# Attention block on eight cores: another order of loads and projections at the start, roots of the last stage on VectorE and GpSimd, and another treatment of the last four token tiles

## The reference

```python
x = x + layernorm(attention(layernorm(x)))     # q, k, v, output projection Wp with bias bp
x = x + layernorm(layernorm(x) @ W[idx] + b[idx])   # idx = argmax(log_softmax(logits) + gumbel(u))
```

## Time and profile before

| | us |
|---|---|
| three timed runs: median (lowest to highest) | 788.21 (786.87 to 789.79) |
| the profiled execution | 792.3 |
| span of its slowest core, core 4 | 791.3 |
| spans of the eight cores | 775.4 to 791.3 |
| busy on core 4: TensorE, VectorE, ScalarE, GpSimd | 691.6, 432.2, 516.2, 116.3 |

### The profile page before, as it was taken

The page is one execution under the profiler, slowest core; times in us unless marked ns, Lnnn a source line. Parts: engine busy times, 40 slices in busy tenths (PEclk is TensorE's granted clock), DMA queues, the critical chain, the costliest instruction groups (busy, mean ns, idle before and its releaser), DMA issues.

```text
span 791.3 us, 17031 instructions; the slowest of 8 cores (775.4 to 791.3 us)
## 1 busy us (share of the span) xinstructions
PE 691.6 (87%) x5700; PEld 259.0 (33%) x5700; DVE 432.2 (55%) x778; ACT 516.2 (65%) x686; POOL 116.3 (15%) x214
## 2 busy tenths in 40 slices
PE   1679999999899999999999998999999999994663
PEld 1344333434333343333333332323233333331221
DVE  4162666664655463452432323476767677674597
ACT  2243126534488687888787888888888888884011
POOL 0110002122211311212111142011011011001000
PEclk9978888888899999999999999999999999998797
DMA  8798247735056132122400064212222322322122
GB/s 204 140 190 171 64 99 198 166 78 148 23 142 148 55 91 63 29 52 45 92 16 15 16 121 109 81 31 78 82 81 69 93 77 76 108 81 88 66 61 93
DMA packets 78627, 72.00 MB, mean 91 GB/s; under 512 B 58448, under 2 KB 60752, under 8 KB 78544
## 3 DMA queue, kind: packets, MB, share of 16 engines
q1 hardware_dynamic: 71856, 59.77, 28.1%
q0 software_dynamic: 6688, 11.14, 8.9%
HBM read 60.68 MB, written 8.52 MB: 87 GB/s over the span
## 4 chain that ended last, share of the span: by engine, by line
PE 61%; issue 14%; ACT 9%; DVE 7%; DMA 6%; POOL 1%; SPq 1%; ACTq 0%; DVEq 0%; POOLq 0%
PE sps L630 10%; PE pj L587 10%; PE pj L571 10%; PE yps L663 10%; ACT Pr L1006 8%; PE pj L580 8%; PE pj L606 4%; PE pj L615 4%; PE zps L681 4%; DMA zr<-zev 2%; DMA wkb<-wk 1%; DMA zscr<-zi 1%; DMA zb<-zscr 1%; DVE Vsb L729 1%; DVE xst L852 1%
## 5 line engine op out<-in xcount | busy, mean ns | idle before, releaser
L1006 ACT ACTIVATE Pr<-sps,negc 128x1024 bf16<-128x1024 f32 (+1 forms) x416 | 429.8, 1079 | 111.3 <-PE sps L632 107.7
L1051 POOL TENSOR_TENSOR Pr<-Pr,mk_sb 128x172 bf16<-128x172 bf16 x192 | 100.3, 543 | 530.0 <-ACT Pr L1006 529.9
L630 PE MATMUL sps<-QY,Ksb 64*128 64x512 bf16 (+2 forms) x480 | 137.7, 348 | 17.9 <-ACT Pr L1006 15.7
L632 PE MATMUL sps<-QY,Ksb 64*128 64x512 bf16 (+2 forms) x480 | 139.3, 352 | 0.0
L663 PE MATMUL yps<-Pr,Vsb 128*32 128x512 bf16 (+5 forms) x1920 | 126.6, 351 | 4.7 <-POOL Pr L1051 2.6
L606 PE MATMUL pj<-wpb,QY 128*128 128x512 bf16 x256 | 68.1, 397 | 16.7 <-DVE QY L820 11.4
L681 PE MATMUL zps<-Pr,cbf 128*32 128x512 bf16 (+2 forms) x960 | 82.2, 347 | 0.0
L630 PEld LDWEIGHTS sps<-QY,Ksb 64*128 64x128 bf16 x480 | 35.7, 94 | 124.9 <-issue 122.2
L580 PE MATMUL pj<-fmQ,wqb 128*128 128x512 bf16 x256 | 67.6, 414 | 1.3 <-ACT Ksb L985 0.7
L729 DVE TENSOR_TENSOR Vsb<-pj,bvb 128x512 bf16<-128x512 f32 x48 | 33.0, 687 | 57.6 <-PE pj L587 52.8
L571 PE MATMUL pj<-fmA,wkb 128*128 128x384 bf16 x256 | 56.1, 370 | 9.2 <-DMA wkb<-wk 6.0
(11 more groups left out here) (93 smaller groups left out, 681.1 us busy)
## 6 DMA issues: line engine op xcount, KB each, us to landing
xin<-xkv SPq DMA_DIRECT2D x21, 512.0 KB, 4.2
zb<-zscr SPq DMA_DIRECT2D x64, 128.0 KB, 2.9
xr<-xq SPq DMA_DIRECT2D x16, 512.0 KB, 3.4
out<-xr SPq DMA_DIRECT2D x16, 512.0 KB, 2.8
xin<-xq SPq DMA_DIRECT2D x12, 512.0 KB, 4.5
wkb<-wk POOLq DMA_DIRECT2D x2, 1024.0 KB, 16.0
wqb<-wq POOLq DMA_DIRECT2D x2, 1024.0 KB, 20.3
wvb<-wv POOLq DMA_DIRECT2D x2, 1024.0 KB, 18.2
```

The source lines that it names most:

```text
L630: PE.matmul(sps[s % 2][:, 0, off:off + w], Ksb[0:64, g, hp, kc:kc + 128], QY[0:64, t, hp, n0:n0 + w], start=True, stop=True, tile_position ...
L632: mm = PE.matmul(sps[s % 2][:, 1, off:off + w], Ksb[64:128, g, hp, kc:kc + 128], QY[64:128, t, hp, n0:n0 + w], start=True, stop=True, tile ...
L1006: A.activation(out=Pr[:, s % 4, :, 0:wide], in_=sps[s % 2][:, :, 0:wide], func=AF.Exp, bias=negc[:, k:k + 1], scale=0.125).then_inc(s_exp, 1)
L1051: op = G.tensor_tensor(out=view, in0=view, in1=mk[:, j:j + 1, :].broadcast_to([128, 2, BAND]), op=ALU.mult)
```

## The change

Lead: `wk` comes in row halves; `wv` is issued when token tile 3 has landed and `wq` when tile 6 has; tiles 3 to 5 are issued after `wk`, tiles 6 to 9 after `wv`. The units' order is K, eight V units, Q, four V units, and the lead's units rotate over four banks (`pj`, `yps`, `zps`). Last stage, tiles 0 to 11: the three roots of each tile are made from a bit guess (three one-column operations on VectorE) and three Newton steps (nine one-column operations on GpSimd). End, tiles 12 to 15: each has a pair of PSUM banks of its own; the biases enter the product as one more matmul from rows that GpSimd splits into bf16 parts; the seven chunks of O that need no last head are multiplied ahead; statistics and the residual read PSUM; `ln3` and the last pass are done on ScalarE; the store is made in halves. The last head's row sums go through ScalarE's DMA queue, and `zinv` and `ynorm` stand later in their lists.

```diff
-    out = t[:3] + k0[:2] + t[3:4] + k0[2:4] + t[4:5] + k0[4:6] + t[5:6] + k0[6:]
-    out += k1[:1] + t[6:7] + k1[1:3] + t[7:8] + k1[3:4] + [("N", "K", 0, 0)] + k1[4:5] + t[8:9] + k1[5:7] + t[9:]
-    out += k1[7:] + [("N", "K", 0, 1)] + q[:4] + [("N", "K", 1, 0)] + q[4:] + [("N", "K", 1, 1)]
-    out += v[:2] + [("N", "Q", 0, 0)] + v[2:5] + [("N", "Q", 0, 1)] + v[5:8] + [("C", 0)] + v[8:]
+    v0, v1 = [[("V", g, sc, eh) for sc in range(3) for eh in range(2)] for g in (0, 1)]
+    nk, nq = [("N", "K", g, h) for g in range(2) for h in range(2)], [("N", "Q", 0, h) for h in range(2)]
+    out = t[:3] + k0[:4] + t[3:4] + k0[4:6] + t[4:5] + k0[6:] + t[5:6] + k1[:3] + nk[:1] + k1[3:] + nk[1:2]
+    out += v0[:2] + t[6:7] + nk[2:3] + v0[2:4] + t[7:8] + nk[3:] + v0[4:] + t[8:9] + v1[:2] + t[9:]
+    out += q + v1[2:3] + nq[:1] + v1[3:4] + nq[1:] + v1[4:5] + [("C", 0)] + v1[5:]
...
-    end = o[12] + o[13] + o[14] + f[12] + o[15] + f[13] + f[14] + f[15]
-    return mid, end
+    return mid
...
-    ln = {i: 5.0 + 2.7 * i for i in range(10)}
+    ln = {i: [5.5, 8.2, 12.0, 26.0, 28.5, 31.0, 44.0, 47.0, 50.0, 53.0][i] for i in range(10)}
+    come = {("K", 0, 0): 20.0, ("V", 0, 0, 0): 44.0, ("Q", 0, 0): 60.0}
...
-    ln.update({10 + i: end["Q", 0, 7] - 2.0 + 4.0 * i for i in range(4)})
-    ln.update({14 + i: end["V", 1, 1, 1] + 4.0 * i for i in range(6)})
+    ln.update({10 + i: end["Q", 0, 7] + [-10.0, -7.0, -1.0, 2.0][i] for i in range(4)})
+    ln.update({14 + i: end["Q", 0, 7] + 6.0 + 4.0 * i for i in range(6)})
...
+    for i, s in enumerate(TAIL):
+        pe.append((NP + 2.0 + 0.1 * i, "tailo", s))
+        pe.append((NP + 3.0 + 0.1 * i, "tailf", s))
...
+                pool.append((x + 1.2 + 4.0, "zroot", u[1]))
+                dve.append((x + 1.2 + 5.5, "x1", u[1]))
+                pool.append((x + 1.2 + 10.0, "x1root", u[1]))
+                dve.append((x + 1.2 + 11.5, "ln3", u[1]))
...
+        by, late = (sp, 1.35) if k < 31 else (act, 1.0)
+        by.append((x + 1.4, "zrow", k))
+        dve.append((x + 4.2 * late, "zinv", k))
+        by.append((x + 4.6 * late, "zout", k))
+        by.append((x + 7.6 * late, "zback", k))
+        again = begin[LAST[k + 2] + 2] - 0.3 if k < 29 else begin[NP] + 20.0
+        dve.append((min(x + 13.5 * late, again), "ynorm", k))
...
+    at = begin[NP] + 16.0
+    z_at, x_at, f_at, last_at = [0.0, 1.4, 5.2, 9.0], [2.8, 6.6, 10.4, 12.8], [15.2, 18.6, 22.0, 26.0], [17.4, 21.0, 24.5, 28.3]
+    for j, s in enumerate(TAIL):
+        dve.append((at + z_at[j], "tailz", s))
+        act.append((at + z_at[j] + 1.4, "tailzroot", s))
+        dve.append((at + x_at[j], "tailx", s))
+        act.append((at + x_at[j] + 2.4, "tailln", s))
+        sp.append((at + x_at[j] + 4.5, "turn", s))
+        dve.append((at + f_at[j], "tailfs", s))
+        act.append((at + f_at[j] + 1.4, "tailfroot", s))
+        dve.append((at + last_at[j], "taillast", s))
+        act.append((at + last_at[j] + 0.6, "tailout", s))
+        sp.append((at + last_at[j] + 1.2, "tailstore", s))
+    for i in range(3):
+        pool.append((begin[FIRST[30]] + 1.0 + 9.0 * i, "biasrow", i))
...
+def bank_number(u):
+
+    return (UNIT_N[u] - 1) % (4 if UNIT_N[u] <= LEAD else 2)
...
+    tail_ps = [pjs[:], sps[0][:], sps[1][:], yzs[:]]
+
+
+    lead_banks = pj + [yps, zps]
...
+    def guess(st, sem_g, n):
+
+
+        V = nc.vector
+        V.tensor_scalar(out=st[:, 14:15], in0=st[:, 13:14], scalar1=EPS, scalar2=0.5,
+                        op0=ALU.add, op1=ALU.mult).then_inc(sem_g, 1)
+        V.wait_ge(sem_g, 3 * n + 1)
+        V.tensor_scalar(out=st[:, 15:16].bitcast(I32), in0=st[:, 14:15].bitcast(I32), scalar1=1, scalar2=None,
+                        op0=ALU.arith_shift_right).then_inc(sem_g, 1)
+        V.wait_ge(sem_g, 3 * n + 2)
+        V.tensor_scalar(out=st[:, 15:16].bitcast(I32), in0=st[:, 15:16].bitcast(I32), scalar1=-1.0,
+                        scalar2=float(0x5f3759df - (1 << 22) - (1 << 31)),
+                        op0=ALU.mult, op1=ALU.add).then_inc(sem_g, 1)
...
+        def tail_begin(s, eh):
+
+            bank = tail_ps[s - 12][:, eh, :]
+            PE.matmul(bank, bsel[:], brow[0][:, 512 * eh:512 * eh + 512], start=True, stop=False)
+            for c in range(7):
+                PE.matmul(bank, QY[:, 3, c, 128 * (s - 12):128 * (s - 11)],
+                          wpb[:, c, 512 * eh:512 * eh + 512], start=False, stop=False)
+
+        def tail_end(s, eh):
+            PE.matmul(tail_ps[s - 12][:, eh, :], QY[:, 3, 7, 128 * (s - 12):128 * (s - 11)],
+                      wpb[:, 7, 512 * eh:512 * eh + 512], start=False, stop=True).then_inc(s_ot, 1)
+
+        def tail_o(s):
+            if s == 12:
+                PE.wait_ge(s_brow, BROWS)
+                PE.wait_ge(s_ynorm, 31)
+                for u in UNITS[-2:]:
+                    ev_sem, ev_n = evicted(u)
+                    PE.wait_ge(ev_sem, ev_n)
+            if s == 13:
+                PE.wait_ge(s_exp, 2 * NP - 1)
+            if s == 14:
+                PE.wait_ge(s_exp, 2 * NP)
+            if s == 15:
+                PE.wait_ge(s_ycopy, 32)
+                PE.wait_ge(s_zcopy, 32)
+            tail_begin(s, 0)
+            if s < 15:
+                tail_begin(s, 1)
+            else:
+                PE.wait_ge(s_ynorm, 32)
+                for r in (12, 13, 14):
+                    tail_end(r, 0)
+                    tail_end(r, 1)
+                tail_end(15, 0)
+                tail_begin(15, 1)
+                tail_end(15, 1)
...
+        def tail_f(s):
+            PE.wait_ge(s_turn[s % 2], 16 * (s // 2 + 1))
+            for eh in range(2):
+                bank = tail_ps[s - 12][:, eh, :]
+                PE.matmul(bank, bsel[:], brow[1][:, 512 * eh:512 * eh + 512], start=True, stop=False)
+                for c in range(8):
+                    mm = PE.matmul(bank, ln3T[s % 2][:, c, :], wfb[:, c, 512 * eh:512 * eh + 512],
+                                   start=False, stop=(c == 7))
+                mm.then_inc(s_ft, 1)
...
+        def tail_x(s):
+            j = s - 12
+            x, st = xr[s % 4][:].rearrange("p (a f) -> p a f", a=2), tst[:, j, :]
+            V.wait_ge(s_tzroot, j + 1)
+            V.wait_ge(s_res[s % 4], 16 * (s // 4 + 1))
+            V.scalar_tensor_tensor(out=x, in0=tail_ps[j], scalar=st[:, 15:16], in1=x,
+                                   op0=ALU.mult, op1=ALU.add).then_inc(s_tx, 1)
+            V.tensor_tensor(out=st[:, 48:49], in0=st[:, 12:13], in1=st[:, 15:16], op=ALU.mult).then_inc(s_tx, 1)
+            V.wait_ge(s_tx, 2 * j + 1)
+            for eh in range(2):
+                V.bn_stats(out=st[:, 16 + 6 * eh:22 + 6 * eh], in_=x[:, eh, :]).then_inc(s_txbn, 1)
+            V.wait_ge(s_txbn, 2 * j + 2)
+            V.bn_aggr(out=st[:, 28:30], in_=st[:, 16:28]).then_inc(s_txst, 1)
+            V.wait_ge(s_txst, 2 * j + 1)
+            V.tensor_scalar(out=st[:, 49:50], in0=st[:, 28:29], scalar1=-1.0, scalar2=None,
+                            op0=ALU.mult).then_inc(s_txst, 1)
...
+        def tail_last(s):
+            j, x = s - 12, xr[s % 4]
+            V.wait_ge(s_tfroot, 3 * j + 1)
+            for eh in range(2):
+                half = x[:, 512 * eh:512 * eh + 512]
+                V.scalar_tensor_tensor(out=half, in0=tail_ps[j][:, eh, :], scalar=tst[:, j, 47:48], in1=half,
+                                       op0=ALU.mult, op1=ALU.add).then_inc(s_tfin, 1)
...
+            A.activation(out=ln3t[s % 2][:], in_=xr[s % 4][:], func=AF.Identity, bias=st[:, 50:51],
+                         scale=st[:, 31:32]).then_inc(s_tln, 1)
...
+        def newton(st, w, n, sem_it, sem_root):
+
+            y, half = st[:, 15:16], st[:, 14:15]
+            for i in range(3):
+                if i > 0:
+                    G.wait_ge(sem_it, 8 * n + 3 * i)
+                G.tensor_tensor(out=w, in0=y, in1=y, op=ALU.mult).then_inc(sem_it, 1)
+                G.wait_ge(sem_it, 8 * n + 3 * i + 1)
+                G.tensor_scalar(out=w, in0=w, scalar1=half, scalar2=-1.5, op0=ALU.mult, op1=ALU.add
+                                ).then_inc(sem_it, 1)
+                G.wait_ge(sem_it, 8 * n + 3 * i + 2)
+                step = G.tensor_tensor(out=y, in0=y, in1=w, op=ALU.mult)
+                if i < 2:
+                    step.then_inc(sem_it, 1)
+                else:
+                    step.then_inc(sem_root, 1)
...
+            G.wait_ge(s_zgs, 3 * s + 3)
+            newton(zst[:, s % 2, :], newt[:, 0:1], s, s_zit, s_zroot)
...
+            n, b, row, rest = 6 * i, (bpb, bfb)[i], brow[i], brest[i]
+            G.wait_ge((s_bp, s_bf)[i], 16)
+            if i == 0:
+                G.wait_ge(s_unit, UNIT_N["O", 7, 1])
+            else:
+                G.wait_ge(s_brow, 6)
+            G.tensor_copy(out=row[:], in_=b[:]).then_inc(s_brow, 1)
+            G.wait_ge(s_brow, n + 1)
+            G.tensor_tensor(out=rest[:], in0=b[:], in1=row[:], op=ALU.subtract).then_inc(s_brow, 1)
```

(17 more changed lines are left out.)

306 lines of the change are left out of this document (223 added, 83 removed).

## The result

| | us |
|---|---|
| three timed runs after: median (lowest to highest) | 814.48 (811.52 to 816.74) |
| the same of before | 788.21 (786.87 to 789.79) |
| ratio, with its 95% interval | 1.0329 (1.0268 to 1.0391) |

What follows compares the result with a forecast made beforehand. TensorE was taken to set the pace, waiting mainly for ScalarE's exponentials. Lead minus 10, heads plus 3 and end minus 18 summed to minus 25 us: median 763 us from 788.21, range 750 to 779.

Steps and rivals of the forecast that it cites:

- (3) of the heads: Last stage: nine GpSimd steps make a root cost 3.3 us, about 0.5 us late, 18 us of waits; plus 3.
- the heads: The stages of attention heads between lead and end: six numbered terms, together plus 3 us.
- slower than before: Rival: GpSimd's root chain bounds the last stage from a step of about 0.54 us; 817 us at 0.6; chance 0.06.
- (1): Heads: 36 roots leave ScalarE, so TensorE waits less for exponentials; minus 5 us (0 to 7).
- (2): Heads: VectorE gets three one-column operations a root, 0.8 us each root, 29 us in all.
- (4): Heads: masks queue behind roots on GpSimd, 0.6 us a head; plus 5 us (0 to 20).
- (5): Heads: two bias rows on GpSimd, 9 to 18 us each, delay roots queued behind them; plus 2 us.
- (6): Heads: later places of divisions and ynorm free VectorE from standing on DMAs in earlier stages; minus 2 us.
- The lead: Before attention: load waits (2.46 + 4.67) and bank waits (5.0) go, less a new stall; minus 10 us (0 to minus 12).
- The stall on `fmQ`: Lead to first stage: with Q last, the next stage's first units wait for fmQ; 2 to 3 us.
- the loads set the lead: Rival: wv or wq lands 5 us late, so the lead gives nothing; 773 us; chance 0.16, counting an end that gives half.
- The end: After the last head: early matmuls, fewer VectorE passes, split store end the span at 773.0 us; minus 18 us.

Runs made afterwards that it cites:

- act_roots_guess: Changed kernel with last-tile roots back on ScalarE, VectorE still making its three guess operations a root into unread columns: 779.88 us, 0.9877 of before.
- late_readers: Changed kernel with VectorE's readers of a root later in its order (x1 and final by 2, ln3 by 4 us): 823.72 us, 1.0423 of before.
- free_roots: Changed kernel with roots on ScalarE, then left out altogether, VectorE using the variance instead: 764.73 us, 0.9663 of before.
- before_again: The kernel before the change, unchanged, run once more for a second profile: 789.61 us, 0.9998 of before.
- norm_back: Changed kernel with ScalarE's roots, the old lead, and zinv and ynorm back at their old places: 773.51 us, 0.977 of before.
- act_roots: Changed kernel with the last tile's 36 roots back on ScalarE and without VectorE's guess operations: 769.36 us, 0.974 of before.

## Why the prediction was wrong

**The failed step is (3) of the heads**, "VectorE asks for a root 3 to 4 us after the statistics, and 0.8 of that is now the guess, so a root comes about 0.5 us late: 18 us of waits", and what follows from it, "VectorE's work of 179 and those 18 leave 25". The price of the root was right, 3.3 us, and so was the guess, 0.15 an operation. But those 3 to 4 us were the nominal distance in the planner. VectorE's real work between guess and reader is 1.1 us for a z root, so it stands 2.3 us there on average, and the waits for roots are 60 us in place of 18. The second error is in the same step: that VectorE's time in waits for units is free. `act_roots_guess` shows that 29 us of work in it cost 8, and `late_readers` that VectorE's waits for units and for roots trade places without a gain: 14 us less of waits for roots (60 to 46), 20 more for units, and a stage that is 9 us longer. This second error weighs more, since fewer stands alone won nothing, while shorter roots did (21 us for the third step). And the sum had no term for the clock, some 8 us by TensorE's busy time. Plus 3 was forecast for the heads; the last stage alone took plus 42.

The rival *slower than before* named the mechanism, and put its threshold at a step of 0.54 us; it came at 0.37. With one step a root, 1.1 us, the loss is 10 against ScalarE; with two 22. There is no cheap side of the threshold, as the guess has spent the gain.

(1), minus 5 for ScalarE: right in kind, `free_roots` gives 7. TensorE's waits for exponentials fell by 4.3 us, from 11.7 (480 to 722 us) to 7.4 (480 to 770). (2), the guesses: the duration was right, their cost of 8 us was taken as nothing. (4), masks, plus 5: the wait is there, 18 us, but taking it away wins 2. (5), bias rows, plus 2: 11, since the first row's `froot` was due at once; a row takes about 10 us, as the lower half of the bound said. (6), minus 2: some 4.

**The lead**, minus 10: nothing was won. Two of its terms fail. The stall on `fmQ` was forecast as 2 to 3 us and is 5.8. And of the 12.1 us of waits that were to go, only those for banks went. Both kinds of wait for loads stayed, as core 0 of after shows:

```profile
25.21 4.00 PE L667 MATMUL pj<-fmA,wkb 128*128 128x384 bf16 x12 [5.06 <-DMA wkb<-wk]
37.03 0.61 PE L650 MATMUL sps<-cbf,tok 128*128 128x128 bf16 x8 [4.17 <-DVE tok L871]
```

Other waits came in place of those for banks, for ScalarE's copies and VectorE's squares (`ksq`) above all:

```profile
76.33 3.61 PE L676 MATMUL pj<-fmQ,wqb 128*128 128x512 bf16 x16 [1.37 <-ACT fmQ L1159]
96.19 0.40 PE L689 MATMUL yz<-ksq,cbf 128*32 128x512 bf16 x4 [2.00 <-DVE ksq L903]
```

From the first K unit to attention TensorE stood 15.4 us on this core, against 12.9 on core 4 of `before_again` at a granted clock of 0.95 (3.4 for the second half of `wkb`, 3.1 for a token tile, 6.5 for banks and small copies). That attention was to start 10 us earlier, at 104 on core 4, was besides a comparison with a core that was at 0.81: on core 4 of `before_again` it starts at 102.33 without any change. The rival *the loads set the lead* gave the lead nothing too, but by late weights; `wvb` and `wqb` were in time (TensorE has no wait on them on core 0), so its mechanism was not it.

**The end**, minus 18: right. It is 16 us shorter by the copies (67.7 to 51.7), and `norm_back`, which has the new end and the old lead and places, takes 0.977 of the time before, 18 us less. Of TensorE's 56 early matmuls the first eight took 3.3 us (761.54 to 764.80), where the granted clock was still at its lower level; the others took 1.73 us for eight (765.16 to 766.89, with the bias row's), 0.22 each as forecast:

```profile
765.16 1.68 PE L790 MATMUL pj<-wpb,QY 128*128 128x512 bf16 x7
766.67 0.38 PE L788 MATMUL sps<-brow,bsel 128*128 128x512 bf16 x1
766.89 1.67 PE L790 MATMUL sps<-wpb,QY 128*128 128x512 bf16 x7
```

So the sum was minus 10, plus 3, minus 18, and what came is about 0, plus 42 less 4, and minus 16: plus 22. The mean of the eight spans rose by 19.8 (784.6 to 804.4). The slowest core of after, core 0, has besides a stage before the last of 170 us, against 161 on core 4 of before; that comes of a stand which four cores of one die had in each execution (below), and not of the change. The version that keeps what paid, the new end and the later places, with the old lead and ScalarE's roots, is `old_lead`: 768.49 us, 0.9733 of before.

Open: how the 42 divide beyond 8 for the guesses, 11 for the bias rows and 30 for the three kinds alone. These overlap, since each was taken alone, and each of them holds a share of the 8 us of clock.

## What to carry to other kernels

Before a short operation is moved to another engine, measure for its reader the work that stands between in its engine's order, not the nominal distance in a planner: what the new way takes beyond that is a stand, once for each use. Moving the reader back does not help by itself when the buffers on its way are single (`late_readers`). A wait for a neighbour is not free time if the neighbour waits for buffers that this engine empties. And read a stage on all cores, with its granted clock, before a gain is counted on the slowest.

## What was not expected of the hardware

- A one-column float32 operation on GpSimd took 0.19 to 0.20 us (product) or 0.27 us (two-operation form) with 0.14 to 0.17 us to the next that depends on it; an Ln on ScalarE took 0.29. Nine in a row are 3.2 us, against one Ln and one Exp.
- A 1,024-column float32 subtraction on GpSimd took 2.39 and 2.91 us for 128 partitions and 2.12 for 64, a cast 1.04. Beside the one of 2.91 VectorE's operations took 1.96 in place of 1.28 us, and 2.07 in place of 0.21. The Trainium skill, "SBUF — State Buffer", section "Who interferes with whom", says that a VectorE instruction with two SBUF inputs contends with a GpSimd instruction that reads SBUF, and that the pair of ports which the two share is an exclusive lock. The trace agrees: the one-column operation has two SBUF inputs, and it ended at 702.36 us, when the subtraction did (702.34).
- The stage before the last took 159 to 165 us on some cores and 166 to 179 on others, in every kernel here. From 440 to 480 us, `act_roots`, core 0 and then core 4:

```profile
440.00:480.00 40.00, 34.27 (x354) 11.55 (x357) 12.06 (x26) 34.52 (x36) 14.16 (x20) 1.00 0.65 147
...
440.00:480.00 40.00, 30.79 (x287) 9.49 (x285) 8.88 (x21) 28.17 (x30) 8.35 (x14) 0.87 0.43 101
```

The granted clock was 0.87 on one, so that TensorE was at its lower level of 1.2 GHz for part of the stretch, and 1.00 (2.4 GHz) on the other. The clock is only the second half of it. On core 4 ScalarE stood first, and TensorE behind it:

```profile
445.62 4.14 ACT L1210 ACTIVATE Pr<-sps,negc 128x1024 bf16<-128x1024 f32 x4 [6.88 <-remote]
446.88 0.58 PE L729 MATMUL sps<-QY,Ksb 64*128 64x512 bf16 x1 [5.87 <-ACT Pr L1210]
```

On core 0 TensorE's longest stand in the whole stage is 0.7 us. In every profile here, before and after, ScalarE's longest stand in this stage was 4.0 to 16.2 us on the four cores of one die, mostly at 443 to 463 us, and 1.4 to 4.6 us on those of the other, and the four are those with the longer stage. Mostly the profile names something outside the core as what ended the stand; what that was is open. Stand and clock together are 10 us of the slowest core, as much as any term of the lead.
